# Eight chained stages: shorter lags in the middle feed-forward, its normalisation roots ahead of its sums, and small-head attention fills one batch later

## The reference

```
x = x + tanh(g_xattn[i]) * attention_i(layernorm(x), ctx)
x = x + tanh(g_ffn[i])   * feed_forward_i(layernorm(x))
```

## Time and profile before

| | us |
|---|---|
| median of 3 runs | 1191.88 (1190.95 to 1194.29) |
| profiled execution | 1197.41 |
| its span | 1195.7 |
| TensorE busy | 1115.3 (93%) |
| VectorE busy | 739.4 (62%) |
| ScalarE busy | 693.5 (58%) |
| GpSimd busy | 474.8 (40%) |
| mean granted TensorE clock | 0.961 of full |

### The profile page before, as it was taken

One profiled execution on the slowest core, in us unless ns is written; L12 is line 12 of the kernel. 1 busy time (PEld: TensorE's weight loads), 2 busy tenths in 40 slices (PEclk: granted clock), 3 DMA queues, 4 the chain that ended last, 5 costly groups with the idle time before them and its releaser, 6 DMA issues. The chain is left out here.

```text
span 1195.7 us, 24475 instructions
## 1 busy us (share of the span) xinstructions
PE 1115.3 (93%) x9865; PEld 813.1 (68%) x9865; DVE 739.4 (62%) x1385; ACT 693.5 (58%) x1225; POOL 474.8 (40%) x737
## 2 busy tenths in 40 slices
PE   4987999899999999999999889998979998999998
PEld 2554367788888888888887557663647764466667
DVE  7663446565556556666565259995658995645554
ACT  3664631366656665666666467777447777644440
POOL 6763001223332333344444454431573543644441
PEclk8885899999999999999999899999979999999999
DMA  9200000100000000000000100000000000033320
GB/s 348 74 2 1 0 1 1 72 1 2 2 1 2 1 1 2 1 2 1 1 2 1 53 1 2 2 3 1 1 1 2 2 2 2 7 98 98 95 81 18
DMA packets 13889, 29.52 MB, mean 25 GB/s; under 512 B 2737, under 2 KB 5073, under 8 KB 13010
## 3 DMA queue, kind: packets, MB, share of 16 engines
q1 hardware_dynamic: 13778, 27.96, 6.9%
HBM read 25.14 MB, written 1.25 MB: 22 GB/s over the span
## 5 line engine op out<-in xcount | busy, mean ns | idle before, releaser
L1242 POOL TENSOR_TENSOR work<-work 128x1024 f32<-128x1024 f32 x64 | 121.3, 1896 | 267.0 <-DVE work L1336 267.0
L1323 DVE TENSOR_REDUCE work<-psum 128x8 f32<-128x1024 f32 x64 | 78.1, 1220 | 86.4 <-PE psum L1122 86.4
L1264 ACT ACTIVATE work<-work 128x1024 f32<-128x1024 f32 x64 | 67.4, 1053 | 95.8 <-DVE work L1327 95.8
L1334 DVE TENSOR_REDUCE work<-work 128x8 f32<-128x1024 f32 x64 | 77.4, 1210 | 70.7 <-ACT work L1264 70.7
L1692 PEld LDWEIGHTS psum<-w_down,work 128*128 128x128 f32 x768 | 99.4, 191 | 28.7 <-issue 27.2
L1692 PE MATMUL psum<-w_down,work 128*128 128x128 f32 x768 | 100.6, 275 | 0.7 <-DVE x L1809 0.7
L981 ACT ACTIVATE work<-psum 128x512 f32<-128x512 f32 x128 | 72.8, 596 | 37.5 <-PE psum L848 36.6
L848 PEld LDWEIGHTS psum<-ident,work 128*128 128x128 f32 x512 | 57.3, 143 | 44.9 <-ACT work L978 25.0
L1021 DVE TENSOR_REDUCE work<-psum 128x8 f32<-128x1024 f32 x64 | 75.2, 1216 | 15.1 <-PE psum L834 14.7
L848 PE MATMUL psum<-ident,work 128*128 128x128 f32 x512 | 76.1, 282 | 7.5 <-ACT work L981 5.9
L1327 DVE TENSOR_TENSOR work<-psum,work 128x1024 f32<-128x1024 f32 x64 | 78.4, 1225 | 6.4
(11 more groups left out here) (336 smaller groups left out, 2558.8 us busy)
## 6 DMA issues: line engine op xcount, KB each, us to landing
work<-chosen SPq DMA_DIRECT2D x80, 128.0 KB, 2.9
x<-in_x SPq DMA_DIRECT2D x2, 512.0 KB, 4.4
ctx_tok<-in_ctx SPq DMA_DIRECT2D x2, 512.0 KB, 6.3
xnt<-in_xt SPq DMA_DIRECT2D x1, 1024.0 KB, 8.3
ctxt<-in_ctxt SPq DMA_DIRECT2D x1, 1024.0 KB, 10.4
mask<-in_mask SPq DMA_DIRECT2D x1, 1024.0 KB, 10.6
w_down<-in_down SPq DMA_DIRECT2D x1, 1024.0 KB, 7.8
ctx_tok<-in_g SPq DMA_DIRECT2D x1, 1024.0 KB, 4.7
```

Of the source, the lines that this page charges most:

```text
L1242: pool.tensor_tensor(prob[:, u % 2, h, :], prob[:, u % 2, h, :], rinv[:, u % 2, h].unsqueeze(2).broadcast_to([P, 8, P]), ALU.mult)\
L1264: act.activation(p, p, ACT.Exp).then_inc(S["exp"], 1)
L1323: dve.tensor_reduce(nmax[:, u % 2, h], s, AX.X, ALU.max, negate=True).then_inc(S["max"], 1)
L1334: dve.tensor_reduce(rsum[:, u % 2, h], prob[:, u % 2, h, :], AX.X, ALU.add).then_inc(S["sum"], 1)
```

## The change

Four edits:

1. In the small-head attentions the fills of the next group stand in the iterations 2, 3, 4 (6, 7, 8; 10, 11, 12) in place of 1, 2, 3 (5, 6, 7; 9, 10, 11).
2. In all feed-forwards GpSimd's program yields behind its whole loop, so all its roots stand ahead of the next stage's head.
3. In that loop a root stands ahead of the pair sum of the same step.
4. f2's lags are (2, 5, 7) in place of (4, 7, 8): roots at m = 13, 21, 29, 37, scalings at 16, 24, 32, 40, turns at 18, 26, 34, 42. The turn of group 2 is thereby ahead of the yield at 35.

```diff
@@ small_head_attention
     def fills(b):
 
-        g, r = divmod(b, GB)
-        return (g + 1, r - 1) if 1 <= r <= 3 and g + 1 < NG else None
+        g, r = divmod(b - 2, GB)
+        return (g + 1, r) if b >= 2 and r < 3 and g + 1 < NG else None
 
@@ tensor
                 if at := fills(b):
                     if b >= 3:
                         pe.wait_ge(S["added"], b - 2)
-                    elif b == 1:
+                    else:
                         prev.ready(pe, NG - 1)
@@ feed_forward, gpsimd
         for m in range(N + LAG + TURN + 1):
-            if m == N - 1 + LAG:
-                yield
-            if one_down and m < N and m % 2:
-                sum_pair(m)
             for n, (_, g1) in enumerate(roots):
                 if not last_sub and m == last(g1 - 1) + ROOT:
                     reciprocal_root(n)
+            if one_down and m < N and m % 2:
+                sum_pair(m)
+        yield
@@ f2
-            return feed_forward(k, prev, "f2", 5, up2, ACT.Silu, ahead=12, lags=(4, 7, 8), on_act=True, one_down=True,
+            return feed_forward(k, prev, "f2", 5, up2, ACT.Silu, ahead=12, lags=(2, 5, 7), on_act=True, one_down=True,
```

## The result

The changed kernel takes 1193.59 us (median of 20 runs), the kernel before 1190.36 in 20 runs beside it: ratio 1.0028, 95% interval 1.0021 to 1.0034, so 2.5 to 4.0 us slower, +3.3 by the ratio. Forecast was +1.5.

A forecast was written before the change was run, and what follows sets the result against it. VectorE's pace of 6.50 us per batch was taken as the limit in a3, and in a2 except iterations with fills. a2 +1.1 and a3 +0.4 gave +1.5 on 1191.88: 1193.4 us, range 1189.3 to 1197.0 (8 in 10).

The forecast's parts named there:

- f1's last root ahead of a2's head: Handover f1 to a2: the root delays `keys(0)` and TensorE's first products; +1.28 us at batch 0, from +1.1 to +1.7.
- clock rival: Rival, chance 0.20: longer waits lower TensorE's clock, costing 1.05 in a2's head and a3's 1.95 gain; sum +4.5, 1196.4 us.
- f2's chain: End of f2: root in series with pair sums in last two groups; last `down` +1.1, bounds -3.0 and +2.2.
- f2's last root ahead of a3's head: Handover f2 to a3: root ahead of `keys(0)` delays TensorE's products; +2.0 us at batch 0, including the 1.1 of f2's chain.
- Fills in a2: a2: iteration 1 loses a fill, -0.99; later iterations where fill and pair's turn meet cost +0.84, between +0.4 and +1.1.
- Fills in a3: a3, batch 1 to 2: iteration 1 loses its fill, gain 1.95 us, between 0.95 and 1.95; later iterations nothing.
- a3's first gather: a3: TensorE's first gather perhaps not quite done, so a3 taken as +0.4 instead of +0.05, between 0 and +1.2.
- The waits and the order: Signs: f2's `down`s wait on GpSimd's sum, not TensorE on scaling at group 1's turn; last root ahead of `keys`.
- doing nothing: Rival, chance 0.13: handover costs and iteration 1's gain cancel, whole kernel 1191.9 us.
- Clock for the worse: The clock rival, chance 0.20: lower TensorE clock in the heads of a2 and a3; sum +4.5, 1196.4 us.
- Clock for the better: Rival, chance 0.13: without the 3.01 us stall TensorE keeps full clock in a3's head, 2.1 off; sum -0.6, 1191.3 us.
- The drain gains: Rival, chance 0.12: f2's pair sums are in time, whole 3.0 us stall saved; sum -2.6, 1189.3 us.

The follow-up runs named there:

- warm runs: e8 and e12, the runs with unread TensorE products added in attention heads; ratios to the kernel before 1.0000 and 0.9972.
- e1: Kernel before with only the fills one iteration later in both attentions; 1190.06 us against 1191.11, ratio 0.9993.
- e3: Kernel before with only f2's roots ahead of pair sums and lags (2, 5, 7), the yield in its old place; ratio 1.0000.
- e4: Kernel before with only the fills of group 1 moved, to iterations 2, 3, 4; ratio 0.9980.
- e2: Kernel before with only GpSimd's yield moved behind its whole loop; 1193.83 us against 1191.11, ratio 1.0023.
- e6: Changed kernel with the fills left in their old iterations; ratio to the kernel before 1.0041.
- e5: The changed kernel itself, measured again against the kernel before; 1193.18 us against 1191.09, ratio 1.0012.
- e7: Changed kernel with the pair sum ahead of the root of the same step; ratio to the kernel before 1.0063.
- e10: Kernel before with f1's lags (1, 4, 5) and the output bias addition one iteration later; 1189.85 us against 1190.84, ratio 0.9987.
- e9: Kernel before with f2's lags (4, 8, 10) and the output bias addition one iteration later; 1187.38 us against 1190.84, ratio 0.9975.
- e8: Changed kernel with unread TensorE products, 3 before and 2 behind `score(0)`, in a2's and a3's heads; 1190.85 us, ratio to the kernel before 1.0000.
- e12: Kernel before with e9, e10 and e4 combined, plus unread products around `score(0)` in a3's head; 1186.88 us against 1190.84, ratio 0.9972.

## Why the prediction was right, and where its terms were off

It held the time in its range, the sign, and the class (slower, but inside 0.3%). That the 1193.4 lies within 0.2 of the measured 1193.59 is luck: it stands on the median of 3 runs, 1191.88, which the 20 runs put at 1190.36, and this 1.5 made up for most of the 1.8 by which the difference was forecast too small. Each term against the table, with means over the runs that share the code in question (warm runs left out):

- *f1's last root ahead of a2's head, +1.28.* 6.14 without (before, e1, e3, e4), 7.48, 7.49, 7.49, 8.17, 8.15 with it (after, e2, e6, e5, e7): mean +1.6. The wait on GpSimd is +1.35 as worked out. In two of five the first products also fell to the lower clock, which is the first half of the clock rival (1.05 there, 0.7 here).
- *f2's chain, +1.1.* 39.81, 40.75, 39.10, 40.76, 39.10 (before, e1, e4, e2, e10) against 41.04, 41.08, 41.03, 41.07 (after, e3, e5, e6): +1.15. The series of statistics, root and sums is shown by TensorE's waits. That the old lags vary by 1.7 with the same code, and the new ones by 0.05, the prediction did not see: in three of the five the clock falls to the lower level in this stretch (granted 0.96), before behind the 3 us stall; in e4 and e10 it stays at 1.00, as it does in all four with the new lags. At equal clock the chain costs 41.05 - 39.10 = 1.95, and the forecast of 1.1 fits because the profile that it was read from, 39.81, lay 0.7 above that.
- *f2's last root ahead of a3's head, +0.9 beyond the downs.* 7.62, 6.78, 7.37, 7.31 against 8.43, 7.60, 8.43, 7.49 (after, e5, e6, e7): +0.7.
- *Fills in a2, -0.99 + 0.84 = -0.15.* From batch 1 to 15, 93.1 (before, e2, e3, e6, e9, e10) against 92.9 (after, e1, e4, e5, e7): -0.2. Both halves were too large: where iteration 1 of a2 ran at the full clock it took 6.69 to 6.78 with the fill (e2, e3, e6) and 6.22 without (after, e1), 0.5 in place of 0.99. The 7.49 held some lower clock (0.90). The sum was right.
- *Fills in a3, -1.95.* This is the term that was mis-sized. The step "8.45 - 1.91 = 6.54, so I take 1.95" read one profile's lower clock (0.78) as the fill's price. With the fill the distance was 8.45, 6.90, 7.05, 8.06, 8.06, 7.51, mean 7.7; without it 7.00, 8.28, 6.47, 6.48, 6.63, 6.86, mean 7.0: -0.7, a difference of two widely spread sets. Between executions with the lower clock for equally long it is -1.05 (e6), just inside the smaller end of 0.95 that the prediction gave.

Sum of the measured terms: 1.6 + 1.15 + 0.7 - 0.2 - 0.7 = +2.5 (+2.2 with -1.05 for the last), 1.0 above the forecast, most of it the fill in a3. (The forecast held 0.35 besides for a3's first gather, which no run shows by itself.) f3 would have to be counted too: its 209.8 and 208.4 look like chance in the first pair, but all five profiles with the late yield and no unread products (after, e2, e5, e6, e7) have the shorter value, and all five with neither the late yield nor lags (4, 8, 10) (before, e1, e3, e4, e10) the longer. If the change brings this -1.3, the sum is +1.2. So of the +3.3 (2.5 to 4.0) of the 20 runs 0.8 to 2.4 us stay open. The edits run alone give 0.9993 x 1.0023 x 1.0000 = 1.0016, between the two measurements of the whole (1.0028 and 1.0012).

Two things point at the clock, without showing it. The mean granted clock is 0.969 at the median of the changed kernel's 20 runs and 0.973 in the 35 runs of the kernel before beside e1 to e4: by an estimate from these, 74 us at the lower level against 64. The first profile pair had it the other way (0.961 before, 0.969 after) and so made the change look too cheap. But e1 and e4, no slower than before, have 0.970 as well, so this share alone is no price. And how often the kernel before took 39.1 or 40.8 in f2, which is worth up to 0.8, can't be read from runs without a profile.

Of the signs that were named, the distances from batch 1 to 2 were to be near 6.5 in both attentions: they were 6.22 and 7.00, the second halfway to the 7.5 that would have spoken against the prediction. The waits and the order were as named.

The rivals: *doing nothing* is excluded by the first 20 runs, though not by e5's 12. *Clock for the worse* happened in part: a2's first products ran at the lower clock in e5 and e7. The time that it takes in a3's first batches is shown by e8, but before pays it too. *Clock for the better* came in f2 (1.00 with the new lags) and not in a3's head: the clock from 885 to 892 was 0.50 again. *The drain gains* did not come: TensorE's `down`s waited 1.31 and 1.72 for the sums. By the Trainium skill (TensorE: Matmul & The Clock Gate, The HAM clock gate) idling throttles and activity releases the throttle; e8 agrees, with 1.00 in place of 0.50, and so does e12.

## What to carry to other kernels

At a handover between stages look first at what stands ahead of the next stage's first need on every in-order queue; moving the old stage's roots ahead of the next one's head cost 2.7 us here, moving a scaling behind it shortened the heads by 1.2 and 2.6. A chain put ahead of work that another engine consumes is free only while that engine has other work; follow it into the drain. A distance read at the lower TensorE clock is a draw, not a price: take it from several profiles of the same code, and compare those in which the lower clock lasted equally long. And work that only keeps TensorE busy must stand behind everything that another engine waits for: in e12 and in e8's a2 the clock was granted in full, and the delay of a turn took the gain back.

## What the runs showed of the hardware that I had not expected

- Identical code in f2 took 39.10 to 40.76 us from first to last `down` (before, e1, e2, e4, e10), and a3's batch 1 to 2 took 6.47 to 8.28 without a fill. The granted clock in these stretches differs from execution to execution: 1.00 (e4, e10) or 0.96 in f2, 0.89 (e4) to 0.63 (e1) in a3.
- From a3's last maxima to the end the profiles show two values, 209.7 to 209.8 or 208.4 to 208.5, and nothing between: in the slower one two pairs of products in f3's head take 1.86 and 1.91 (before) in place of 1.13 and 1.02 (after). Which kernel has which is told above; why is open.
- With unread products in a3's head the granted clock was 1.00 from batch 0 to 2 (e8, e12); the twelve profiles without them had 0.50 to 0.79 from batch 0 to 1.
